# Edge messages of a graph layer: three 64-column products into one set of PSUM columns, scaled by ScalarE out of PSUM, without the VectorE join

## What is computed

```python
for _ in range(3):
    x = jax.ops.segment_sum(vals[:, None] * x[cols], rows, num_segments=18750)
    acc = acc + x
light_out = acc / 4
...
rating = users_emb @ items_emb.T + bias_user[users] + bias_item.T
return jax.nn.sigmoid(rating)
```

## Time and profile before

| | us |
|---|---|
| median of three runs | 7039.1 |
| span of the profiled execution (first to last instruction) | 6215.1 |
| rest of the time, outside the span | 824.0 |
| first half, layer 0: first to last scatter issued | 1064.0 |
| the same, layer 1 | 875.5 |
| the same, layer 2 | 869.3 |

### The profile page before, as it was taken

The page is one execution under the profiler, slowest core; times in us unless marked ns, Lnnn a source line. Parts: engine busy times, 40 slices in busy tenths (PEclk is TensorE's granted clock), DMA queues, the critical chain, the costliest instruction groups (busy, mean ns, idle before and its releaser), DMA issues.

```text
span 6215.1 us, 180067 instructions
## 1 busy us (share of the span) xinstructions
PE 4166.1 (67%) x58894; PEld 3693.3 (59%) x58895; DVE 5208.7 (84%) x7771; ACT 4176.2 (67%) x10330; POOL 2389.9 (38%) x2110
## 2 busy tenths in 40 slices
PE   5400211115777777899766777799867677699979
PEld 4400111105676667899766666799856666699944
DVE  9999999997777777899977777799987777799950
ACT  0055565425656655899777777799867777799966
POOL 0044334204666666100177777300067777600000
PEclk9855555556888887999898888899989889899979
DMA  9600000004666666666476666666567667666636
GB/s 333 263 4 0 0 0 0 0 7 136 176 175 180 177 176 179 156 160 160 120 193 191 196 192 194 168 160 160 129 174 195 192 195 196 178 159 160 159 115 241
DMA packets 741330, 924.82 MB, mean 149 GB/s; under 512 B 71016, under 2 KB 586889, under 8 KB 741147
## 3 DMA queue, kind: packets, MB, share of 16 engines
q1 hardware_dynamic: 648172, 669.17, 41.4%
q0 software_dynamic: 92672, 254.01, 11.1%
q10 hardware_dynamic: 434, 1.05, 0.1%
HBM read 532.77 MB, written 391.26 MB: 149 GB/s over the span
## 4 chain that ended last, share of the span: by engine, by line
PE 43%; DVE 29%; issue 12%; DMA 9%; ACT 5%; DVEq 1%; POOL 0%; POOLq 0%; SPq 0%; ACTq 0%
PE psum L1553 15%; DMA posts<-ring 9%; PE psum L1547 8%; PE psum L1516 7%; DVE ring L1221 4%; DVE ring L1265 4%; DVE store L1029 4%; ACT ring L660 4%; PE psum L1518 3%; DVE store L1027 3%; DVE total L857 3%; PE psum L1500 3%; DVE store L1047 3%; PE psum L1542 2%; DVE store L1048 2%
## 5 line engine op out<-in xcount | busy, mean ns | idle before, releaser
L775 POOL DMA_INDIRECT posts<-ring x1920 | 1970.2, 1026 | 2212.0 <-ACT ring L660 1716.1
L660 ACT ACTIVATE ring<-ring 128x64 f32<-128x64 f32 x7680 | 1918.3, 335 | 920.4 <-DVE ring L1221 901.0
L1516 PE MATMUL psum<-store,ring 128*128 x15360 | 1852.2, 239 | 739.2 <-DVE ring L1265 658.9
L1516 PEld LDWEIGHTS psum<-store,ring 128*128 128x128 bf16 x15360 | 1568.5, 110 | 864.8 <-issue 838.0
L1518 PE MATMUL psum<-store,ring 128*128 x15360 | 1760.0, 210 | 0.0
L1518 PEld LDWEIGHTS psum<-store,ring 128*128 128x128 bf16 x15360 | 1461.3, 106 | 47.0 <-issue 0.2
L1221 DVE TENSOR_REDUCE ring<-psum 128x512 f32<-128x1024 f32 x960 | 1171.9, 1221 | 313.1 <-PE psum L1518 299.8
L1553 PE MATMUL psum<-ring 128*128 128x64 bf16 x15168 | 998.8, 225 | 1.1 <-DVE ring L1303 1.1
L1553 PEld LDWEIGHTS psum<-ring 128*128 128x128 bf16 x15168 | 959.5, 166 | 8.2 <-DVE ring L1303 1.5
L1265 DVE TENSOR_SCALAR ring<-ring,lane_f 128x1024 bf16<-128x1024 bf16 x1920 | 872.6, 496 | 15.5 <-DMA ring<-lanes_d 15.3
L758 POOL TENSOR_TENSOR ring<-store 128x1024 f32<-128x1024 f32 x157 | 370.2, 2358 | 811.3 <-DVE store L1048 375.2
(11 more groups left out here) (252 smaller groups left out, 4551.4 us busy)
## 6 DMA issues: line engine op xcount, KB each, us to landing
ring<-lanes_d SPq DMA_DIRECT2D x480, 512.0 KB
ring<-posts SPq DMA_DIRECT2D x240, 516.0 KB
store<-posts SPq DMA_DIRECT2D x234, 516.0 KB, 3.9
out<-ring SPq DMA_DIRECT2D x200, 250.0 KB, 2.0
posts<-store SPq DMA_DIRECT2D x2, 20640.0 KB, 115.8
posts<-store SPq DMA_DIRECT2D x2, 20124.0 KB, 88.7
posts<-ring POOLq DMA_INDIRECT x1920
ring<-runs_d SPq DMA_DIRECT2D x80, 256.0 KB
```

The source lines that it names most:

```text
L660: last = nc.scalar.activation(of, of, ACT.Copy, scale=vring[:, h, c * BLOCK + b:c * BLOCK + b + 1])
L775: pool.indirect_dma_start(out=posts[:, :], out_offset=bass.IndirectOffsetOnAxis(ap=dring[:, h, c:c + 1], axis=0), in_=msg[:, n, :], in_off ...
L1516: pe.matmul(psum[:, c, b * 2 * F:(b + 1) * 2 * F], of, xflat[:, bass.ds(at_d[c] * F + k * XT, 2 * F)], start=(k == 0), stop=False, skip_gr ...
```

## The change

TensorE runs three matmuls of 64 columns per one-hot instead of one of 128 and one of 64, one per part, and all three (and both k) accumulate into the same 64 PSUM columns. A chunk then fills half a bank and a duo one bank; four banks rotate by duos. ScalarE reads the finished sums from PSUM and writes the scaled message into its slot, so it waits for TensorE (`s_sent`) directly. The join and its semaphore go. TensorE waits, before it writes a bank again, until ScalarE has scaled the duo of four duos ago (`s_msg`).

```diff
@@ ScalarE, for each chunk n of a body
                         if n % 2 == 0:
-                            act.wait_ge(s_added, i * 8 + (layer * DUOS + n // 2 + 3))
+                            act.wait_ge(s_sent, i * 8 + (layer * DUOS + n // 2 + 3))
                         for b in range(BLOCK):
-                            of = msg[:, n, b // 2 * HROW + b % 2 * F:b // 2 * HROW + b % 2 * F + F]
-                            last = nc.scalar.activation(of, of, ACT.Copy,
+                            last = nc.scalar.activation(msg[:, n, b // 2 * HROW + b % 2 * F:b // 2 * HROW + b % 2 * F + F],
+                                                        psum[:, n // 2 % 4, (n % 2 * BLOCK + b) * F:(n % 2 * BLOCK + b + 1) * F], ACT.Copy,
                                                         scale=vring[:, h, c * BLOCK + b:c * BLOCK + b + 1])
                         last.then_inc(s_msg, 1)
@@ VectorE
-                def join(sent, d):
-
-                    dve.wait_ge(s_sent, sent)
-                    sums = psum[:, d % 2 * 2:d % 2 * 2 + 2, :].rearrange("p s (a e x f) -> p (s a) e f x", a=2, e=2, x=2)
-                    nc.vector.tensor_reduce(msg_sums[:, d, :, :].rearrange("p a (e f) -> p a e f", f=F), sums, AX.X, ALU.add).then_inc(s_added, 1)
-
@@ VectorE, send
                             dve.wait_ge(s_sent, i * 8 + (layer * DUOS + d + 1))
-                            if not (first and d < 2):
-                                join(i * 8 + (layer * DUOS + d + 1), (d + 6) % 8)
@@ VectorE, after the loop
-                for d in range(2):
-                    join((layer + 1) * DUOS + d + 1, 6 + d)
-
@@ TensorE, sums
                         if n % 2 == 0:
                             pe.wait_ge(s_hots, i * 8 + (layer * DUOS + d + 5))
-                            pe.wait_ge(s_added, i * 8 + (layer * DUOS + d + 1))
+                            pe.wait_ge(s_msg, i * 16 + (done + 2 * d + 10))
                         for b in range(BLOCK):
+                            to = psum[:, d % 4, (n % 2 * BLOCK + b) * F:(n % 2 * BLOCK + b + 1) * F]
                             for k in range(2):
                                 of = hot[d % 2][:, k, n % 2 * CHUNK + b * P:n % 2 * CHUNK + (b + 1) * P]
-                                pe.matmul(psum[:, c, b * 2 * F:(b + 1) * 2 * F], of, xflat[:, bass.ds(at_d[c] * F + k * XT, 2 * F)],
-                                          start=(k == 0), stop=False, skip_group_check=True)
-                                last = pe.matmul(psum[:, c, (2 * b + 1) * F:(2 * b + 2) * F], of, xflat[:, bass.ds(at_d[c] * F + (k * XT + 2 * F), F)],
-                                                 start=False, stop=(k == 1), skip_group_check=True)
+                                for x in range(PARTS):
+                                    last = pe.matmul(to, of, xflat[:, bass.ds(at_d[c] * F + (k * XT + x * F), F)],
+                                                     start=(k == 0 and x == 0), stop=(k == 1 and x == PARTS - 1), skip_group_check=True)
@@ TensorE, end of the first half
-                pe.wait_ge(s_added, (layer + 1) * DUOS + 2)
+                pe.wait_ge(s_msg, (layer + 1) * CHUNKS + 16)
```

More of the change, by code:

```diff
@@ L199, in build @@
         msg = ring[:, 4096:4096 + 16 * ROW].rearrange("p (s w) -> p s w", w=ROW)
-        msg_sums = ring[:, 4096:4096 + 16 * ROW].rearrange("p (d a w) -> p d a w", a=4, w=HROW)[:, :, :, 0:2 * F]
         msg_lanes = ring[:, 4096:4096 + 16 * ROW].bitcast(BF16).rearrange("p (s a w) -> p s a w", a=2, w=2 * HROW)[:, :, :, 4 * F:2 * HROW]
@@ L338, in build @@
         s_msg = sem("s_msg")
-        s_added = sem("s_added")
         s_scat = [sem(f"s_scat{h}") for h in range(2)]
@@ L1177, in _ @@
             dve.sem_inc(s_msg, 16)
-            dve.sem_inc(s_added, 2)
             dve.sem_inc(s_unit, 2)
```

## The result

| | before | after |
|---|---|---|
| median of the runs, us | 7036.9 (7024.3 to 7044.8, 4 runs) | 7188.3 (7185.4 to 7190.0, 4 runs) |
| ratio, with its 95% interval | | 1.0211 (1.0195 to 1.0227) |

A forecast was written before the change was run, and what follows sets the result against it. GpSimd's scatters were taken to bound layers 1 and 2, VectorE with TensorE layer 0. Gains of 80 + 20 + 18 + 4 = 122 us took 7039.1 to 6917, rounded to 6920 us (1.7% faster); range 6820 to 7045 us.

The forecast's parts named there:

- The time outside the span: Whole kernel: 824.0 us were taken to lie outside the profiled span of 6215.1 us and carried over unchanged.
- What bounds the kernel: First halves: GpSimd's scatters with 0.305 us gaps fill 97% of layers 1 and 2; layer 0 couples VectorE and TensorE.
- Layers 1 and 2, 20 and 18 us: First halves of layers 1 and 2: removing the join cuts GpSimd's waits, at most 27 and 23 us, taken as 20 and 18.
- Layer 0, 80 us (bounds 136 and 0): Layer 0's first half: removing the join gains 80 us, with TensorE's stream then setting the pace; 136 if all at full clock.
- the 984 us: Layer 0's first half after the change: forecast length, 80 halves of a body at mixed TensorE clock.
- the forecast's own 11.6 and 13.1: Layer 0, TensorE's time per half of a body: 11.6 us at full clock, 13.1 us at half clock.
- TensorE's cadence: TensorE's stream: 64-column matmuls 28 ns apart, six register computations of 0.126 us per chunk, 1.97 us per duo.
- The prediction's check on the old duo: TensorE, kernel before: a duo's 32 matmuls took 1.60 us, explained as 4 at 0.13 and 28 at 0.043.
- ScalarE: ScalarE's 7680 copies, now out of PSUM: no change from 0.25 us each, 1.0 us per chunk.
- The time at the layers' starts, 4 us: Start of each layer: the first message leaves one join earlier, 3 x 1.2 = 4 us gained.
- The rivals: Four alternative outcomes for the whole kernel: 6781 us (chance 0.08), 6997 us (0.10), 7279 us (0.12), 7039 us (0.08).
- Rival (c): TensorE: weight loads of 42.5 ns set the pace, a duo takes 2.85 us, kernel slower at 7279 us; chance 0.12.

The follow-up runs named there:

- before_short: Kernel before with TensorE's loop body in layers 1 and 2 halved to 8 chunks; on the quiet chip (before: 6235.6 us) 6235.3 us, ratio 1.0004.
- after_short: Changed kernel with TensorE's loop body in layers 1 and 2 halved to 8 chunks; on the quiet chip (before: 6235.6 us) 6181.4 us, 0.9907 of before.
- three_join2: Kernel before with three matmuls of 64 columns per one-hot and the join kept, on a usual chip (before: 7039 to 7115 us); 7718.6 us, 1.0954 of before.

## Why the prediction was wrong

**The time outside the span: the step that failed.** "7039.1 = 6215.1 + 824.0" carried 824.0 us over as time outside the span. In every later run it was 2 us. The rows thus came from an execution of some 6217 us, as on the quiet chip, as its halves show (1062, 880 and 880 us there against 1064.0, 875.5 and 869.3), and the timed ones were like those of the usual chips, on which the first halves have another bound. All that follows was argued for a case that the metric doesn't measure.

**What bounds the kernel.** For the quiet chip it was right: GpSimd paces layers 1 and 2, and four different kernels stay within 873 to 882 us. On the usual chips TensorE is held up by the scatters, the halves of before take 1175 and 1181 us, and GpSimd itself waits.

**Layers 1 and 2, 20 and 18 us.** On the quiet chip 7 and 5 us (before_short to after_short, 880.2 to 873.6 and 880.1 to 874.9). That is no more than two executions of the kernel before differ by (875.5 and 880.2, 869.3 and 880.1), and the halves stay above the 850 to 860 us of the forecast. The step that failed here is that the join's removal would take 20 and 18 us off GpSimd's waits. Beyond 0.305 us per scatter it stood idle for 34 and 36 us in before_short and for 33 and 34 in after_short. These waits are nearly all in six pauses, 112 scatters apart: 27.7 us in layer 1 of the rows' execution, 34.8 in after_short. No run shows what makes them. Besides, the first scatters of a layer, which now lie closer beside the `take` additions, last longer: in after_short

```profile
L773 POOL DMA_INDIRECT posts<-ring x5 | 10.1, 2013 | 560.2 <-ACT ring L657 559.3 <-issue 0.9
```

against a mean of 1199 ns for the first four in the rows' execution. On the usual chips the same halves became 57 and 51 us longer.

**Layer 0, 80 us (bounds 136 and 0).** On the quiet chip 36 us (1061.9 to 1026.2), within the bounds; on the usual ones none (1299.4 to 1315.1). The mechanism was right on the quiet chip: TensorE is the pace there, the join's removal alone gives 109 us, and the third matmul with its register work takes 73 of them. The term that was mis-sized is the stream of a half's four duos. The look-up block takes 3.90 us in after_short, as forecast for the full clock; the four duos take 8.98 us from first to last matmul, with hardly a pause, where the 984 us leave 8.4 for them. The clock is a small part of it: 43% of the time at 1.2 GHz instead of 36 (granted clock 0.78 against 0.82) makes 8 us by the forecast's own 11.6 and 13.1. Most of the remaining 34 us fits a duo that takes 2.15 us at full clock instead of 1.97 (next paragraph); that is an estimate.

**TensorE's cadence.** Right for the single matmul. 64-column matmuls start 29 ns apart at full clock. The register computations are six per chunk (3816 for 636 chunks in layer 1's window):

```profile
L1504 PEldq FUSED_REGOPS  x3816: 46/46/51, 3327.1 to 4550.9; - x191
```

Unheld, a duo takes 2.15 us, where the sum gave 1.97. (The prediction's check on the old duo, "4 at 0.13 and 28 at 0.043", gives 1.72 us and not the 1.60 of the rows.) Where it is held, no such sum applies. The Trainium skill's rule in "TensorE: Matmul & The Clock Gate", section "Back-to-back issue gap", about 81 ns per matmul at 128 columns in a stream with weight loads, is not borne out: in the earlier trace rows a 128-column product with its weight load is followed after 55 ns by the next. The unheld duo has 48 matmuls of 64 columns with their loads in 2.15 us, 45 ns each with all its register work, and so stays under the 62 ns that the prediction quotes as well.

**ScalarE.** I took no change at 0.25 us a copy; it is a little faster out of PSUM, eight in 1.75 us (0.22), and mattered nowhere.

**The time at the layers' starts, 4 us.** Outside the first halves after_short is 5.5 us shorter than before_short, which agrees.

**The rivals.** Together, the quiet chip gave 54 us of the 122 forecast, 0.9% instead of 1.7% (after_short). That the sign was right there is no credit to the forecast, which was made for the timed 7039 us. The usual chips gave 2.1% slower, which none of the rivals describes. Rival (c) has this sign, but through weight loads of 42.5 ns, and the 29 ns exclude it. (The prediction's argument against it, a load that "was done 28 ns later", is not what the trace has: that load's bar lasts 98 ns, and it is the next matmul that starts 28 ns later.) What the prediction counted on to hide TensorE's longer stream, GpSimd's 2.65 us per duo, is just what was turned round: the scatters that were to cover TensorE slow it.

**What stays open.** Why chips differ, or one chip from time to time; by which path an indirect scatter reaches TensorE; why a chain holds it longer than single scatters do; and why some signals pass in the middle of a chain in the kernel before. I have no run on whether scatters that are spaced apart would free a kernel that needs all of them. Of the variants that compute the whole result, none beats the kernel before on a usual chip.

## What to carry to other kernels

Compare the profiled execution's span with the timed runs before anything else: when hundreds of microseconds "lie outside the span", the profile shows another case than the one that is timed, and every bound read from it is conditional. Where an engine is idle with "issue" and its signals are late, look at which neighbour was active, not at its own program, and take the neighbours away one at a time; halves of two alike layers can hold four such trials in one kernel. In a pipeline whose messages leave by indirect scatters one behind the other, the price of a matmul depends on where it falls: the third one cost 673 us with the join kept (three_join2), 221 us without it and 43 to 67 us on the quiet chip.

## What the hardware did that I had not expected

- On the usual chips, in the changed kernel, a chain of four indirect scatters of GpSimd, 0.30 us apart, holds nearly all of TensorE's signals, from 0.8 us after its start until 1.0 us after its end, and slows its matmuls from 19 to 4 starts per us. VectorE and ScalarE go on signalling. In the kernel before as many signals come in the middle of a chain as after it. On the quiet chip there are chains of 112 scatters with little of it: in layer 1 a signal came over 0.3 us late 2 times in 306 in before_short and 29 in 302 in after_short.
- The number of bytes doesn't matter (32 or 1032 per row: 3.85 us per duo with both), nor does the number of rows (64 or 128: 3.91 and 3.85). A plain transfer of 128 rows of 1032 bytes from the same engine does no harm (2.26 us), though it goes through the same software queue. The Trainium skill, "DMA: Bandwidth & Descriptors", section "SWDGE vs HWDGE vs iDMA", describes plain and indirect transfers from GpSimd as made in the same way, with descriptors that GpSimd writes into SBUF. So by the page that writing alone doesn't explain the effect, and no run shows what in the indirect form does.
- With indirect scatters at every other chunk TensorE stood at 2.4 GHz throughout (granted clock 1.00 at 91% busy); held up by them, the same program had 0.70. So the low clock of these halves comes with the pauses, and not from the program of TensorE itself.
- The same program took 6236 us on one chip and 7037 to 7115 us in all other comparisons.
